# A sparse graph attention layer on one Trainium2 core: row sums of a chunk moved to the end of the slot in front, one more s1 row by DMA, and the turn moved between two tiles

## The reference, cut to what matters

```python
def gnn(h, in2, adj, a1, a2):            # h, in2: 4096 x 128; adj: 4096 x 4096 of 0 and 1
    e = h @ a1 + (in2 @ a2).T            # s1 (one per row) + s2 (one per column)
    e = where(e > 0, e, 0.2 * e)
    att = softmax(where(adj > 0, e, -9e15), axis=1)
    att = att * sum(adj, axis=1)
    return (0.1 * att + 0.9 * adj) @ in2
x = x + gnn(layernorm(x), in2, adj, a1, a2)
x = x + layernorm(x) @ weight.T + bias
```

## Time and profile before

| | us |
|---|---|
| median of 3 runs | 380.49 (380.19 to 382.05) |
| the profiled execution | 381.12 |
| its span, first to last instruction | 379.2 |
| TensorE busy | 362.9 |
| VectorE busy | 311.8 |
| ScalarE busy | 247.8 |
| GpSimd busy | 132.1 |

### The profile page before, as it was taken

The page is one execution under the profiler, slowest core; times in us unless marked ns, Lnnn a source line. Parts: engine busy times, 40 slices in busy tenths (PEclk is TensorE's granted clock), DMA queues, the critical chain, the costliest instruction groups (busy, mean ns, idle before and its releaser), DMA issues.

```text
span 379.2 us, 8935 instructions
## 1 busy us (share of the span) xinstructions
PE 362.9 (96%) x3231; PEld 317.8 (84%) x3231; DVE 311.8 (82%) x791; ACT 247.8 (65%) x630; POOL 132.1 (35%) x257
## 2 busy tenths in 40 slices
PE   7789999999999999999999999999999998999991
PEld 6578888888888888888888888888888887888880
DVE  5989989969999488787969687887989788999843
ACT  4799887596935492929477492937768098569210
POOL 4594632606070512506061351706144130401121
PEclk9999999999999999999999999999999999999997
DMA  7999959572936999989896999989675920010000
GB/s 241 210 213 206 217 104 210 101 157 49 203 21 48 216 64 197 17 168 95 108 153 38 219 21 198 65 105 151 100 163 14 192 61 14 16 16 15 3 29 18
DMA packets 19467, 42.06 MB, mean 111 GB/s; under 512 B 4822, under 2 KB 10716, under 8 KB 19420
## 3 DMA queue, kind: packets, MB, share of 16 engines
q0 software_dynamic: 9216, 33.56, 62.2%
q1 hardware_dynamic: 10204, 7.89, 7.5%
HBM read 72.88 MB, written 2.11 MB: 198 GB/s over the span
## 4 chain that ended last, share of the span: by engine, by line
PE 81%; DMA 8%; ACT 4%; issue 2%; POOL 1%; DVE 1%; POOLq 0%; DVEq 0%
PE acc_y L673 26%; PE acc_v L693 21%; PE acc_u L690 21%; PE acc_v L673 4%; PE acc_u L673 3%; DMA adj_all<-adj 3%; ACT steep L494 3%; DMA s_bc<-s_rows 3%; DMA s_rows<-pre_s 2%; PE small L658 2%; PE acc_u L664 1%; PE acc_v L664 1%; PE turned L632 1%; POOL adj_all L358 1%; PE small L644 0%
## 5 line engine op out<-in xcount | busy, mean ns | idle before, releaser
L494 ACT ACTIVATE steep<-s_bc,steep_s 128x256 bf16<-128x256 f32 x512 | 208.0, 495 | 85.0 <-DMA s_bc<-s_rows 75.3
L693 PE MATMUL acc_v<-weights_v,minus 128*128 128x258 f16 x864 | 191.0, 272 | 0.0
L690 PE MATMUL acc_u<-weights_u,plus 128*128 128x258 f16 x864 | 191.0, 273 | 0.0
L673 PE MATMUL acc_y<-weights_y,adj_all 128*128 128x257 f16 x960 | 109.1, 273 | 0.4 <-DMA adj_all<-adj 0.4
L673 PEld LDWEIGHTS acc_y<-weights_y,adj_all 128*128 128x128 bf16 x960 | 93.0, 97 | 13.7 <-DMA adj_all<-adj 0.7
L889 DVE TENSOR_TENSOR plus<-adj_all,steep 128x2048 bf16<-128x2048 bf16 x64 | 78.4, 1225 | 18.1 <-ACT steep L494 17.8
L690 PEld LDWEIGHTS acc_u<-weights_u,plus 128*128 128x128 bf16 x864 | 83.3, 96 | 11.8
L693 PEld LDWEIGHTS acc_v<-weights_v,minus 128*128 128x128 bf16 x864 | 83.9, 97 | 11.1
L892 DVE TENSOR_TENSOR minus<-adj_all,plus 128x2048 bf16<-128x2048 bf16 x64 | 78.4, 1225 | 2.2
L400 POOL TENSOR_SCALAR post_var<-post_mv 128x2 f32<-128x2 f32 x15 | 3.2, 213 | 166.8 <-DVE post_mv L954 166.8
L358 POOL DMA_DIRECT2D adj_all<-adj x64 | 36.0, 582 | 7.1 <-DMA plus<-in 4.6
(11 more groups left out here) (116 smaller groups left out, 327.7 us busy)
## 6 DMA issues: line engine op xcount, KB each, us to landing
adj_all<-adj POOLq DMA_DIRECT2D x64, 512.0 KB, 14.8
x_in<-x SPq DMA_DIRECT2D x16, 128.0 KB, 10.5
plus<-in SPq DMA_DIRECT2D x4, 512.0 KB, 5.9
out<-late SPq DMA_DIRECT2D x15, 128.0 KB, 2.8
s_bc<-s_rows SPq DMA_DIRECT2D x11, 128.0 KB, 8.9
s_rows<-pre_s SPq DMA_DIRECT2D x11, 1.0 KB
out<-late SPq DMA_DIRECT2D x2, 64.0 KB, 2.4
s_rows<-s_bc SPq DMA_DIRECT2D x5, 1.0 KB
```

Of the source, the lines that this page charges most:

```text
L494: ins = nc.scalar.activation(steep[:, h, k, :], s1_bc[b][:, :], ACT.Relu, bias=steep_s2[:, jt:jt + 1], scale=STEEP)
L673: ends[t] = nc.tensor.matmul(acc[t][:, 0:width], left[:, jt, cols(t)], right[:, jt, :, :].rearrange("p a b -> p (a b)")[:, 0:width], start ...
L690: last_u = nc.tensor.matmul(acc_u[t][:, 0:2 * WC], plus[b][:, jt, cols(t)], w_u[:, jt, :, :].rearrange("p a b -> p (a b)"), start=(jt == 0 ...
L693: last_v = nc.tensor.matmul(acc_v[t][:, 0:2 * WC], minus[b][:, jt, cols(t)], w_v[:, jt, :, :].rearrange("p a b -> p (a b)"), start=(jt == ...
```

## The change

One constant goes from 5 to 4. In the two slots before the last that have no Y product (12 and 14) TensorE turns chunk c-1 between the two tiles, and ScalarE copies it between its first numerator and the sign tests of quarters 2 and 3. `pre_start` of a chunk moves from the start of a slot to the end of the one in front, behind `post_start`; only that of chunk 2 stays where it was.

```diff
-SPREAD = 5
+SPREAD = 4
@@ ScalarE, slot
                     [0, 1, "first", "second", "copies", 2, 3] if c == 1 else \
+                    [0, 1, "first", "copies", 2, 3, "second"] if ahead(c, 1) and y_chunk(c) is None else \
                     [0, 1, "first", 2, 3, "second", "copies"] if ahead(c, 1) else \
@@ TensorE, slot
-                    for t in range(TILES):
-                        pe.wait_ge(tile_left, 2 * c + t - 1)
-                        both(t, b, c)
+                    pe.wait_ge(tile_left, 2 * c - 1)
+                    both(0, b, c)
+                    if y_chunk(c) is None:
+                        turn(c - 1)
+                    pe.wait_ge(tile_left, 2 * c)
+                    both(1, b, c)
                     if c + 2 < SPREAD:
                         spread(c + 2, b)
-                    turn(c - 1)
+                    if y_chunk(c) is not None:
+                        turn(c - 1)
@@ VectorE, slot
-                if ahead(c, 2):
-                    pre_start(c + 2, b)
+                if not inner(c):
+                    pre_start(2, 0)
@@
                 post_start(c)
+                if ahead(c, 3):
+                    pre_start(c + 3, 1 - b)
```

## The result

The changed kernel takes 383.69 us (median of 20 runs, 380.31 to 388.94) against 380.87 (379.88 to 382.34) of the kernel before, run beside it: 1.0059 times as long, 95% interval [1.0042, 1.0076]. So it is slower, as forecast, but by 0.6% and not by the 1.5% of the forecast (386.5 us).

A forecast was written before the change was run, and what follows sets the result against it. TensorE, busy 96%, was taken to bound the kernel; a late VectorE moves the turn of slot 15 by 5.8 us. 381.12 + 5.8 = 386.9, taken as 386.5; range 379.5 to 388.8, the forecast's own 383.8 to 388.5.

The forecast's parts named there:

- Spread removed, holes closed: TensorE's slot 2 loses 0.45 us; the holes before the linear products of slots 12 and 14 go, 1.54 and 0.73.
- The hold of slot 2: VectorE's masks hold GpSimd's three small row-sum operations, so the s1 write is issued 4.90 us after `finish` starts.
- The ceiling of 2.72 us: The most TensorE can gain: the spread of slot 2 and the holes of slots 12 and 14 together.
- Slot 3: s1 lands 8.85 us into TensorE's slot 3, over the limit of 7.60; the linear product costs 1.34 us.
- The loop after that: For odd slots, a turn of two slots takes 44.82 us against 43.70; TensorE pays 1.12 in slots 5, 7 and 9.
- The price of two DMAs as a constant: From the s1 write's issue to the next sign tests, two DMAs in a row, taken as 18.5 us.
- starved loads: Rival: the added scattered write delays the adjacency loads; costs only from a delay of 5 us on; chance 0.01.
- The end: VectorE's slot 12 ends 7.1 us later, `xn` of chunk 14 comes at 367.2, the turn of slot 15 5.8 later.
- half held: Rival: write at F + 3.7, one mask; slots 3 to 11 unstalled, `xn` 1.7 later; 382 to 383.5 us; chance 0.15.

The follow-up runs named there:

- the kernel whose masks wait: The changed kernel with VectorE waiting ahead of the masks until GpSimd has made the row sums; ratio 0.9952, median 379.55 us.
- the kernel with the small load: The changed kernel with the adjacency load of chunk 6, loaded in slot 2, cut to an eighth; ratio 0.9966, median 380.02 us.

## Why the prediction was right or wrong

**Spread removed, holes closed**: right. Slot 2 is 0.45 shorter, slot 12 1.45, slot 14 0.59 (forecast 0.45, 1.54, 0.73).

**The hold of slot 2**: right, F + 4.96 for F + 4.90, from the row that stood in slot 14. The ceiling of 2.72 us was right as well: the kernel whose masks wait is 2.7 shorter from its first linear product on (295.2 against 297.9).

**Slot 3**: the mechanism was right, the size too large. The two DMAs took 17.86, not 18.5. Against its slot, which the clock had made late along with it, s1 came 8.2 us in, not 8.85. The stall was 0.64, forecast 1.34.

**"The loop after that"**: this is the step that failed. I had 44.82 us a turn and 1.12 us of stall in slots 5, 7 and 9; there is none (slots 4 to 11: +0.10 together). From slot 3's landing to slot 5's are 42.26 us (113.37 to 155.63). For the even slots between I let s1 of slot 4 come at 128.5, with 18.5 us for its two DMAs. They took 23.12 (111.90 to 135.02). F of slot 4, forecast 133.9, was 134.77, so the sign tests, which should have been 5 us ahead of it, weren't begun. The rows of this kernel give the dependence, with L the start of the sign tests and F that of `finish` in the same slot:

| slot | F - L | write |
|---|---|---|
| 3 | -4.14 | F + 2.67 |
| 4 | -0.25 | F + 2.67 |
| 5 | 1.03 | F + 3.68 |
| 6 | -0.62 | F + 2.66 |
| 7 | 1.30 | F + 3.41 |
| 8 | -1.53 | F + 2.68 |
| 9 | 2.85 | F + 5.05 |
| 11 | 0.48 | F + 2.66 |

A full hold needs the sign tests some 2 us ahead or more (in other kernels 2.15 gave F + 4.61, and 2.27 F + 5.64). Slot 13 is no exception: there they are 5.14 ahead and the write still comes at F + 2.70, but the range check stands between `finish` and the masks, which start only at 330.97, behind the row sums.

A late s1 protects the row sums behind it, so the hold limits itself: it strikes, the chain becomes late, and it can't strike again until the chain has caught up (slot 2, then slot 9). The prediction says as much of slots 4 to 9 before ("there the masks waited for s1") and didn't ask it of its own later slots. What the long write takes, 8 us once, the freed row sums and the loop's slack give back over the next slots. Whether a turn of 44.82 would come about with 18.5 us in slot 3 wasn't seen: in the kernel with the small load the broadcast was early too.

**The price of two DMAs as a constant**: by the sum this is why that step failed. With 18.5 us from 111.90 on, s1 of slot 4 would have come at 130.4, 4.4 ahead of `finish` and early enough for a hold; that is worked out, not run. I read 18.1 to 19.6 off nine pairs (the shortest is in fact 16.92, 261.23 to 278.15, which changes neither the 18.5 nor the lower bound's lack of a stall). None of them had less than 20.3 us from the write in front, and I carried 18.5 to a write that the forecast itself put at 110.0, 16 us behind the one in front (93.95). Moving a transfer earlier in one slot and not in the next brings it into the burst. I had looked at starved loads as a rival, the write delaying the adjacency (it does: the load of slot 2 flows from 106 on, 10.6 us behind its issue and not 2, though TensorE never waits for it), and not at the reverse.

**The end**: the place was right and its cause half so. The turn of slot 15 waits 2.04 for `xn`, which is done at 364.89. I had 367.2 and a turn 5.8 later. The start of slot 13, which waits 1.54 for the emptied tile, I hadn't named. VectorE's slot 12 ends at 326.4 (326.16 + 0.25), forecast 328.6. It is late by what happens in slots 9 and 10, the second hold and the long transfers behind it, and not by a loop that never catches up.

**Sum.** By the profile's own terms: -0.45 - 1.45 - 0.59 + 0.64 + 0.10 + 1.69 + 2.04 = +2.0, near the measured 0.6% (2.2 us); the other 3.3 us of the profiled execution are the clock at the start and behind the last wait, and rounding. The rival "half held" (382 to 383.5) gave nearly the time, but not the mechanism: it had the first write at F + 3.7.

## What to carry to other kernels

A transfer's duration belongs to the moment at which it is issued: before one is moved, lay its new issue time beside the bursts of the queue and see how long they still flow. A small operation on GpSimd that a critical DMA hangs on belongs ahead of VectorE's long two-input operations, by an order or by a wait; 7.3 us of waiting on VectorE, at most 1.6 at a time, bought 4 us here. And a chain of two slots in which lateness itself removes the cause of lateness has no steady loss per turn: follow it slot by slot, with both conditions (which comes last, s1 or `finish`) tested each time.

## What the runs showed of the hardware

A write of 256 values of 4 bytes from a column layout to HBM took 7.4 to 9.8 us in slots 12 and 13 of all kernels, where hardly a load is left. In slot 2 of the changed kernel 4 to 61 GB/s flowed from 96 to 106 us, behind the write, although 2 MB were waiting; in the kernel before, without such a write, the same load flows 2 us behind its issue. Beside a running 2 MB burst it took up to 18.7 us: the remainder of the burst and its own 8. The broadcast of 1 KB to 128 partitions took 3.6 to 5.5 us in slots 12 and 13 of the kernels before and after, and 8.1 to 10.5 in the earlier slots of the kernel before. A wait of 2.0 us of TensorE was followed by a granted clock of 0.68 over 5.4 us in one execution, and by 1.00 in two others.
